# Who makes the high halves of the context tiles: GpSimd or ScalarE, and a set of edits around it in a fused Perceiver kernel

## What is computed

```python
# L0 cross attention: 32 heads of 8, keys and values from the context
q = x @ Wq.T;  kv = context @ [Wk; Wv].T
q = rmsnorm(q); k = rmsnorm(k)                 # over the 8 elements of a head
out = softmax(q @ k.T / sqrt(8)) @ v           # 2048 context rows for each batch
...
# L0 self attention: 16 heads of 128, causal, then w_o
...
# L0 ffn with ternary weights
s = mean(abs(w));  w_t = clip(round(w / s), -1, 1) * s
...
# then: a decayed sum of the context, a linear attention by phases, a mixture of experts
```

## Time and profile before

| | us |
|---|---|
| median of 3 runs | 462.28 (461.65 to 462.77) |
| profiled execution, own time | 462.64 |
| its span, first to last instruction | 460.5 |
| busy: PE / DVE / ACT / POOL | 404.6 / 321.8 / 250.0 / 225.4 |
| cross attention, first to last exp | 20.7 to 183.9 |
| self attention | about 190 to 285 |

### The profile page before, as it was taken

How to read it: one execution, slowest core, us unless ns; L and a number is a source line. 1 busy time by engine, 2 the same in 40 slices (tenths; PEclk the granted TensorE clock), 3 DMA queues, 4 the chain that set the end, 5 groups by cost and what they waited for, 6 DMA issues and landing times.

```text
span 460.5 us, 12543 instructions
## 1 busy us (share of the span) xinstructions
PE 404.6 (88%) x5149; PEld 336.7 (73%) x5149; DVE 321.8 (70%) x674; ACT 250.0 (54%) x494; POOL 225.4 (49%) x269
## 2 busy tenths in 40 slices
PE   6688989999999998769969967789788988999997
PEld 4456667776777776668969966676688877989996
DVE  5887978888988883648898987581899867522221
ACT  4357778878888889265534412530824134544441
POOL 3378657756766741333633540510189852445440
PEclk9889999999999999979998989998989999999999
DMA  4086732532211003600000003910000034000000
GB/s 145 1 310 208 226 124 69 185 92 86 78 36 41 26 3 127 266 0 0 4 0 2 0 2 117 429 81 1 0 1 1 2 137 183 1 0 1 0 2 23
DMA packets 10536, 34.66 MB, mean 75 GB/s; under 512 B 2160, under 2 KB 7280, under 8 KB 8688
## 3 DMA queue, kind: packets, MB, share of 16 engines
q1 hardware_dynamic: 10480, 33.86, 20.9%
HBM read 33.60 MB, written 0.26 MB: 74 GB/s over the span
## 4 chain that ended last, share of the span: by engine, by line
PE 45%; DVE 31%; POOL 11%; issue 6%; ACT 4%; DMA 2%; SPq 0%; DVEq 0%; POOLq 0%; ACTq 0%
PE ps L1067 7%; PE ps L1560 6%; PE ps L1053 5%; PE ps L1516 4%; PE ps L1530 3%; DVE sb_big L1302 3%; DVE sb_big L1300 2%; PE ps L1547 2%; POOL sb_arena L976 2%; PE ps L389 2%; PE ps L738 2%; DVE sb_big L562 2%; DVE sb_arena L1310 2%; POOL sb_mid L990 2%; PE ps L375 1%
## 5 line engine op out<-in xcount | busy, mean ns | idle before, releaser
L1486 ACT ACTIVATE sb_arena<-ps 128x1024 f32<-128x1024 f32 x128 | 123.4, 1021 | 26.0 <-PE ps L1547 26.0
L1560 PE MATMUL ps<-sb_arena 128*25 128x128 f32 (+1 forms) x2048 | 69.1, 275 | 0.0
L1516 PE MATMUL ps<-sb_halves 128*128 128x512 f32 x192 | 54.5, 419 | 2.8 <-POOL sb_halves L1421 1.1
L1560 PEld LDWEIGHTS ps<-sb_arena 128*25 128x25 f32 (+1 forms) x2048 | 50.4, 97 | 7.3 <-ACT sb_arena L1486 0.4
L1097 POOL TENSOR_TENSOR sb_halves<-sb_big,sb_halves 128x704 fp32r<-128x704 f32 x20 | 33.7, 1687 | 38.9 <-ACT sb_halves L1091 38.9
L479 POOL TENSOR_TENSOR sb_halves<-sb_big,sb_halves 128x256 fp32r<-128x256 f32 x32 | 24.2, 779 | 55.6 <-ACT sb_halves L463 55.6
L1516 PEld LDWEIGHTS ps<-sb_halves 128*128 128x128 f32 x192 | 34.2, 192 | 16.1 <-issue 6.5
L1163 DVE SCALAR_TENSOR_TENSOR sb_arena<-ps,sb_w_q,sb_arena 128x176 f32<-128x176 f32 x40 | 15.9, 401 | 42.7 <-ACT sb_arena L1115 42.5
L1067 PE MATMUL ps<-sb_halves 128*128 128x352 f32 x240 | 42.9, 332 | 2.0 <-POOL sb_halves L1097 2.0
L1377 POOL TENSOR_TENSOR sb_big<-sb_arena 128x256 f32<-128x256 f32 x32 | 19.6, 612 | 51.1 <-DVE sb_arena L1274 51.1
L1067 PEld LDWEIGHTS ps<-sb_halves 128*128 128x128 f32 x240 | 39.1, 189 | 3.3 <-DVE sb_arena L1163 1.7
(11 more groups left out here) (220 smaller groups left out, 877.5 us busy)
## 6 DMA issues: line engine op xcount, KB each, us to landing
sb_big<-in_w_gu SPq DMA_DIRECT2D x2, 3520.0 KB, 15.6
sb_arena<-in_ctx SPq DMA_DIRECT2D x32, 128.0 KB, 2.2
sb_mid<-in_w_down SPq DMA_DIRECT2D x1, 3584.0 KB, 12.3
sb_mid<-in_w_ffn SPq DMA_DIRECT2D x3, 768.0 KB, 5.1
sb_big<-in_w_q SPq DMA_DIRECT2D x2, 1024.0 KB, 6.8
sb_big<-in_w_k SPq DMA_DIRECT2D x2, 1024.0 KB, 6.2
sb_big<-in_w_v SPq DMA_DIRECT2D x2, 1024.0 KB, 6.1
sb_mid<-in_w_o SPq DMA_DIRECT2D x2, 1024.0 KB, 5.8
```

The lines of the kernel that those rows point to most:

```text
L1486: nc.scalar.activation(probs[:, n % P_SLOTS].rearrange("p a g n -> p a (g n)"), ps[:, bank:bank + 2], ACT.Exp, scale=XD ** -0.5).then_inc( ...
L1516: i = T.matmul(ps[:, 7], ctx_half[:, t % 2, c, kt], wkv_half[:, d, kt], start=(n + kt == 0), stop=(n == 2 and kt == KT - 1))
L1560: i = T.matmul(ps[32 * gg:32 * gg + m, 6, j * P:(j + 1) * P], v_sb[:, t % V_SLOTS, 4 * gg + j, head], probs[:, n % P_SLOTS, a, gg], start= ...
```

## The change

The high halves of context tiles 0 to 3 are made by POOL, and those of tiles 4 to 31 by ACT, which copies tile t + 3 after the first `exps` of PE tile t. The rest of the edits: the low half of the key and value weights goes from POOL to DVE, and their load to ACT's queue; the packs of queries and keys are a narrow copy, a narrow subtraction and one copy that doubles both; the first squares and the first query copy go to ACT; `project(1)` comes after `turn_queries(0)`; the accumulator is taken in two pieces, and batch 0's is turned in the last tile, in another bank; the layer norm ahead of the self attention is finished batch by batch; ACT takes the three absolute sums ahead of the head loop; a ternary piece is two operations, not three; the first half of the expert weights may be loaded a little sooner.

The core of the diff:

```diff
             def split_context(t):

-                if t >= 2:
-                    pool.wait_ge(sem(f"ctx_loaded{t % CTX_SLOTS}"), 16 * (t // CTX_SLOTS + 1))
-                    pool.wait_ge(sem("kv_projected"), t - 1)
+                pool.wait_ge(sem(f"ctx_loaded{t % CTX_SLOTS}"), 16 * (t // CTX_SLOTS + 1))
+                if t < 4:
+                    if t >= 2:
+                        pool.wait_ge(sem("kv_projected"), t - 1)
                     G.tensor_copy(ctx_half[:, t % 2, 0], ctxT[:, t % CTX_SLOTS]).then_inc(sem("ctx_high"), 1)
                 pool.wait_ge(sem("ctx_high"), t + 1)
                 G.tensor_tensor(ctx_half[:, t % 2, 1], ctxT[:, t % CTX_SLOTS], ctx_half[:, t % 2, 0].bitcast(F32),
...
+            def split_high(t):
+
+                act.wait_ge(sem(f"ctx_loaded{t % CTX_SLOTS}"), 16 * (t // CTX_SLOTS + 1))
+                act.wait_ge(sem("kv_projected"), t - 1)
+                nc.scalar.copy(ctx_half[:, t % 2, 0], ctxT[:, t % CTX_SLOTS]).then_inc(sem("ctx_high"), 1)
...
                 for c in range(SUBS):
                     exps(SUBS * t + c)
+                    if c == 0 and 4 <= t + 3 < NB:
+                        split_high(t + 3)
...
+            dve.wait_ge(sem("wkv_high"), 1)
+            V.tensor_tensor(wkv_half[:, 1], w_xkv, wkv_half[:, 0].bitcast(F32), ALU.subtract).then_inc(sem("wkv_split"), 1)
...
-                kn2 = knb[:, :, None, :].to_broadcast([P, XH, 2, XD])
-                V.tensor_copy(pack[:, :, :, 0], kn2).then_inc(sem("k_high"), 1)
+                V.tensor_copy(pack[:, :, 0, 0], knb).then_inc(sem("k_high"), 1)
                 dve.wait_ge(sem("k_high"), t + 1)
-                V.tensor_tensor(pack[:, :, :, 1], kn2, pack[:, :, :, 0], ALU.subtract
-                                ).then_inc(sem("k_packed"), 1)
+                V.tensor_tensor(pack[:, :, 0, 1], knb, pack[:, :, 0, 0], ALU.subtract).then_inc(sem("k_low"), 1)
+                dve.wait_ge(sem("k_low"), t + 1)
+                halves_of = kpack[:, t % 2].rearrange("p (h s c) -> p h s c", s=2, c=16)
+                V.tensor_copy(halves_of[:, :, 1], halves_of[:, :, 0]).then_inc(sem("k_packed"), 1)
...
+            act.wait_ge(sem("w_ffn"), loaded["w_ffn"])
+            for n in range(3):
+                if n:
+                    act.wait_ge(sem("ffn_abs"), n)
+                nc.scalar.activation(w_abs, w_ffn[:, n], ACT.Abs, accum_out=fsc[:, n:n + 1]).then_inc(sem("ffn_abs"), 1)
...
-                step(dve, V.tensor_scalar(tern, src, fsc[:, w + 9:w + 10], None, ALU.is_lt))
-                step(dve, V.scalar_tensor_tensor(tern, src, fsc[:, w + 6:w + 7], tern, ALU.is_gt, ALU.subtract))
-                V.tensor_copy(w_tern[:, w, s * FCHUNK:(s + 1) * FCHUNK], tern).then_inc(sem("ffn_ternary"), 1)
-                dve.wait_ge(sem("ffn_ternary"), 4 * w + s + 1)
+                n = slice(s * FCHUNK, (s + 1) * FCHUNK)
+                if w + s:
+                    dve.wait_ge(sem("ffn_ternary"), 4 * w + s)
+                step(dve, V.tensor_scalar(below, w_ffn[:, w, n], fsc[:, w + 9:w + 10], None, ALU.is_lt))
+                V.scalar_tensor_tensor(w_tern[w][:, n], w_ffn[:, w, n], fsc[:, w + 6:w + 7], below, ALU.is_gt,
+                                       ALU.subtract).then_inc(sem("ffn_ternary"), 1)
```

More of the change, by code:

```diff
@@ L29 @@
 SUBS = 4
+ACC_BANKS = (7, 5)
 CTX_SLOTS = V_SLOTS = P_SLOTS = 4
@@ L300, in layer_norm @@
                 nc.vector.bn_aggr(mv[:, b], bn[:, b]).then_inc(sem("ln_stats"), 1)
+                if apart:
+                    normalise(b)
             if not normed:
                 dve.wait_ge(sem("ln_stats"), B * (k + 1))
[L303 to L307, removed]
+            for b in range(B if normed and not apart else 0):
+                normalise(b)
         def ln_copy(dve, n, bank):
@@ L321, in split_x, with ln_rstd @@
             nc.vector.tensor_tensor(half[:, 1], t, high, ALU.subtract).then_inc(sem(name + "_low"), 1)
-        def ln_rstd(act, k):
-            for b in range(B):
+        def ln_rstd(act, k, batch=None):
+            for b in range(B) if batch is None else (batch,):
                 act.wait_ge(sem("ln_stats"), B * k + b + 1)
@@ L537, in scalar_attention @@
                                    ).then_inc(sem("pT_taken"), 1)
[L538 to L543, removed]
                 if i + 2 < AH:
@@ L1315, in take_acc @@
                 dve.wait_ge(sem("pv_done"), SUBS * MB * (b + 1))
-                if b == 0:
-                    dve.wait_ge(sem("q_transposed"), B)
-                V.tensor_copy(accs[:, b], ps[:, 6]).then_inc(sem("acc_taken"), 1)
-            decay_rate()
-            mean_squares_q(0)
-            take_kv(0)
-            pack_q(0)
-            mean_squares(0)
-            take_q(0, 4)
-            pack_keys(0)
-            take_kv(1)
-            mean_squares(1)
-            take_keys(0)
-            pack_keys(1)
+                for c in range(2):
+                    V.tensor_copy(accs[:, b, c * 256:(c + 1) * 256], ps[:, 6, c * 256:(c + 1) * 256]
+                                  ).then_inc(sem("acc_taken"), 1)
+            dve.wait_ge(sem("wkv_high"), 1)
+            V.tensor_tensor(wkv_half[:, 1], w_xkv, wkv_half[:, 0].bitcast(F32), ALU.subtract).then_inc(sem("wkv_split"), 1)
+            mean_squares_q(0)
+            take_k(0)
+            norm_q(0)
+            mean_squares(0)
+            pack_q(0)
+            take_v(0)
+            pack_keys(0)
+            take_k(1)
+            take_keys(0)
+            take_v(1)
+            mean_squares(1)
+            pack_keys(1)
+            decay_rate()
             decay_weights(0)
@@ L1487, in exps @@
                                      ACT.Exp, scale=XD ** -0.5).then_inc(sem("exp_done"), 1)
-            for t in range(2):
-                key_rstd(t)
+            key_rstd(0)
+            act.wait_ge(sem("q_transposed"), 1)
+            nc.scalar.copy(qT_x[:, 0], ps[:, 4].bitcast(F16).rearrange("p (g n) -> p g n", g=GROUPS)
+                           ).then_inc(sem("q_ready"), 1)
+            key_rstd(1)
             for t in range(NB):
@@ L1562, in values, with turn_acc @@
                 i.then_inc(sem("pv_done"), 1)
+            def turn_acc(b):
+                for j in range(4):
+                    if j % 2 == 0:
+                        pe.wait_ge(sem("acc_taken"), 2 * b + j // 2 + 1)
+                    i = T.transpose(ps[:, ACC_BANKS[b], j * P:(j + 1) * P], accs[:, b, j * P:(j + 1) * P], id32[:])
+                i.then_inc(sem("acc_transposed"), 1)
             def open_acc():
@@ L1604, in _ @@
                     turn_keys(t + 1)
+                else:
+                    turn_acc(0)
                 scores(2 * t + 1)
```

83 lines of the change are left out of this document (41 added, 42 removed).

## The result

| | before | changed |
|---|---|---|
| median, us | 462.37 (461.65 to 462.77, 4 runs) | 536.68 (533.23 to 540.89, 4 runs) |
| ratio, with its 95% interval | | 1.161 (1.153 to 1.170) |
| profiled execution, own time / span | 462.64 / 460.5 | 540.89 / 539.1 |

The changed kernel is 16% slower, 2.7 us above the 534 that were forecast. The profiled execution is the slowest of the four, 4.2 us above their median, at a mean granted TensorE clock of 0.921; the others had 0.929, 0.929 and, in the fastest, 0.942. From the page of the changed kernel: the span, the busy times, the clock in 40 slices, shares of the chain that ended last, and four groups (line, engine, operation, output<-input, form, count | busy us, mean ns | idle us just before them and what ended most of it).

What follows compares the result with a forecast made beforehand. PE sets the pace at 4.81 us a cross-attention tile; the change makes a wait loop through four engines the bound. 65.6 + 3.2 + 1.6 + 14 - 3 - 1.5 - 8 = +71.9 on 462.64: about 534 us, range 508 to 556.

Steps and rivals of the forecast that it cites:

- The ring: Cross attention: a wait loop through all four engines once a tile, 7.47 us replacing 5.13 in 28 tiles, +65.6 us.
- The two long tiles: Cross attention: extra work inside the loop, +3.2 us for packing batch 1's queries and +1.6 us in PE tile 6.
- The clock: Cross attention: PE's idle pieces bring half speed for a third of the time, +14 us (bounds 0 and 42).
- The rival in which the clock holds: Cross attention: the same loop between engines without the 14 us for half speed, 520 us; chance 0.33.
- the one with half clock throughout: Cross attention: PE at half speed for nearly all of it, 562 us; chance 0.10.
- The start: Kernel start: low half of weights on DVE, first squares and query copy on ACT, weights loaded earlier: -3 us (0 to -5).
- the earlier load: Kernel start: the earlier load of the key and value weights, counted as a gain within the -3 us there.
- The hand-over: Between batches: PE's 2.12 us wait for batch 1's accumulator shrinks as batch 0 is turned in the last tile, -1.5 us.
- The self attention: Head loop: absolute sums made ahead of it give 4.4 us, shorter ternary pieces 3.5; together -8 us (-4 to -11).
- The lighter pack: Cross attention, DVE's narrower pack of keys: worth nothing and costing nothing, because DVE waits for most of the loop.
- the rival in which the copy hides: Cross attention: POOL always finds ACT's copy ready, no loop closes, 4.81 us a tile, 441 us; chance 0.05.
- The rival with the weighing ahead of the wait: Cross attention: POOL weighs before waiting for ACT's copy, the loop is 5.9 us, the time 490 us; chance 0.04.

Runs made afterwards that it cites:

- the run with the weighing first: Changed kernel with POOL's two weighing instructions of a tile put ahead of its low half: 483.22 us, ratio 1.046.
- the added matmuls: Changed kernel plus 20 matmuls that nothing reads, in PE's idle time ahead of the projection of each tile 1 to 28: 529.42 us, ratio 1.142.
- the SP run: Changed kernel with ACT's copy one tile earlier and the load of the key and value weights back on SP's queue: 445.38 us, ratio 0.963.
- the kernel with POOL's copies: Changed kernel with the high halves of all context tiles made by POOL again, other edits kept: 451.68 us, ratio 0.975.

## Why the prediction was right, and where it was not

**The ring** was right, in its length and, to 0.08 us, in each of its steps. 7.47 was forecast; ten tiles take 7.44 to 7.47, and the run with the weighing first shows that its length is the sum of what stands in it. Each of the runs that take the copy out of the loop (on POOL, or one tile earlier) ends below the kernel before.

**The two long tiles.** The packing of the queries was put at 3.2 and took 2.8 (51.20 to 53.96, POOL alone at work). Tile 6 was put at +1.6; its keys come 2.2 us after the mean squares and not 0.34, +1.9.

**The clock** was right in its mechanism and low in its size. Above 28 x 7.46 = 208.9 the 28 tiles spent 23.8 us. Fourteen tiles without extra work of their own lie 13.9 above the ring together; with the added matmuls the same fourteen lie 0.4 above it, so that 13.6 of it is shown to be the clock's. The three tiles with extra work, 3, 6 and 16, lie 10.7 above. The packing is 2.8 of that, the late keys of tile 6 are 1.9, and tile 16 has 0.8 of its own, which the forecast left out: it takes 6.75 us against 5.97 in the kernel with the weighing first, where its clock was full. The 5.2 that are left are inferred to be the clock's from the half-clock rows in these tiles, such as the projection of 2.90 us, and not shown. (Tile 15 took 0.8 less than the ring, since POOL has one weighing operation there and not two.) So the clock cost some 19 us where 14 was forecast, in the slowest of the four executions; the median one is 4.2 us shorter at a higher granted clock.

The price was right: tiles in which the whole projection is at half clock take 8.94, 1.48 above the ring, for the 1.5 that was taken. The share of time was nearly right: 0.83 to 0.87 granted means 26 to 34% at half speed, against a third. In the 25 ordinary tiles share times price would give 12.5, near the 13.9 found. It fails in tiles 3, 6 and 16, behind the longest idle pieces of PE (5.38, 3.94 and 3.04 us), which pay the price in full or more. And it is not the share alone that counts: in tile 1 the clock is low over the turning of the keys (0.97 us from 32.92, and 0.61 to 0.62 at full clock), PE only waits less ahead of the projection (1.44 us, shown above, and 2.61 in many other tiles), and the tile takes 7.47. The rival in which the clock holds is refuted by the half-clock rows, and so is the one with half clock throughout: ten tiles lie at 7.44 to 7.47, with their projections at 1.6.

**The start** is the term with the wrong sign: -3 forecast, +2.3 measured, and two steps of it failed. The first is "the earlier load" as a gain. Only the receiving side was costed, and not that `x`, whose load runs beside this one, is used 1.9 us later for it. With the load back on SP the first exps come at 17.05 us, against 20.74 before, a gain of 3.7. With the load on ACT's queue they come at 20.68 in the changed kernel and at 19.93 in the one that the SP run was built on, alike up to there, so that the early load takes back 2.9 of the 3.7 and most of what is left lies within what such kernels differ by. The second is tile 0, for which the forecast had no term: 10.5 us against 8.1. PE waits 3.43 us in it behind three scans on DVE; moving two of them gave 0.8 us there and cost more ahead of it, so the rest is open. DVE's low half took 1.22 us, near the 1.3 that was taken. To the exps of tile 1 the kernel with the load on SP needs 27.59 us against 28.88 before.

**The hand-over** came as forecast, -1.3 for -1.5: PE's wait for the accumulator is 0.55 us against 2.12. **The self attention** gave 11.6 for 8. From the first projection to the first finished head 5.4 were won (4.4 forecast); the wait of 4.05 us ahead of the third projection is now

```profile
288.51 1.67 PE L395 MATMUL ps<-sb_halves 128*128 128x256 f32 x12 [1.04 <-POOL sb_halves L485]
```

and the stretch from the first to the last finished head is 66.8 us against 72.7, 5.9 for the 3.5 that was put on the shorter ternary; 0.3 lies behind it. PE let through more than the 12 x 0.4 counted. It is not the sums, whose return left this stretch as it was. The granted clock fell twice in it before (from 240.9 and 271.6 us) and once in the changed kernel (from 323.8), which may be part of it; this was not tried.

**The lighter pack** was worth nothing, as forecast, but the reason given holds only in the ring. Outside it the pack gains little too (at most the 1.5 us over 28 tiles of the kernel with POOL's copies), and in the tile that was looked at DVE and POOL slow each other by as much as it saves. That step failed in the rival in which the copy hides: its 4.81 us a tile would have given 134.7, and the kernels without the ring take 141.9 and 142.1.

**Partial opening.** The rival with the weighing ahead of the wait was priced at 5.9 us a tile and 490 us; built, it is 5.97 and 483.2. Its price kept the 14 us for the clock, and the clock was full there in all ordinary tiles. As a forecast of this change it was wrong, as the order said.

The version that beats both kernels is the change with ACT's copy one tile earlier and the weight load left on SP: 445.38 us, 3.7% below the kernel before (0.960 to 0.965).

## What to carry to other kernels

When a producer is moved to another engine, look up what stands ahead of it in the new stream and what stands behind its consumer in the old one: if the first needs this tile's result and the second feeds it, the move closes a ring, and its length is the sum of all steps, however idle the engines are. Add the steps start to start from one tile in the trace; then move the step one tile earlier before giving up the idea. Price a half clock by the work of the chain that it falls on, and count in full the tiles behind the longest idle pieces. Price an earlier load by whom it delays as well.

## What the runs showed of the hardware that was not expected

Two DVE operations on 128x256 elements went from 0.29 and 0.42 us to 0.64 and 0.92 beside POOL's operations, while POOL's went from 0.73 to 1.00. The Trainium skill (SBUF — State Buffer, "SBUF: two separate sides") has it that a GpSimd operation that reads SBUF and a DVE operation with two SBUF inputs, or in a mode that uses both ports, shut each other out for a whole instruction. The trace agrees that both sides are lengthened; whether the cast, which has one input, was in such a mode, no run shows.

And idle pieces of PE well short of the 4.05 us of the earlier trace rows were followed by a fall of the granted clock. It was 0.83 to 0.87 from 20 to 250 us of the changed kernel, where the head loop, with PE busy for 19.5 of 20 us, had 1.00 (the last row of the changed kernel's windows above). From tile 7 to 28 each fall came in or within 1.5 us behind an idle piece of 2.5 to 3.0 us; the pieces of 1.0 to 2.3 us there had none behind them, but they are short because PE's work ahead of them was still at half clock, and so tell nothing of the length that is needed. Ahead of the projection at 72.17 us a piece of 2.61 had none either, so the length of one piece does not settle it. With the weighing first the pieces are 0.8 to 1.6 us from tile 7 on, and the clock was full there.
